# Attention in blocks of four heads: scores in strips of rows, keys copied by DMA, the sink as a column, normalised probabilities, a transposed value product

## What is computed

```python
q = einsum('bqm,muh->bquh', norm(x), Wq) + bq      # 32 heads of 64
k = einsum('bkm,mvh->bkvh', norm(x), Wk) + bk      # 8 heads of 64, each serves 4 query heads
v = einsum('bkm,mvh->bkvh', norm(x), Wv) + bv
q, k = rope(q) * SCALE, rope(k) * SCALE            # (even, odd) pairs are rotated
scores = where(abs(i - j) <= 128, q @ k.T, -1e9)   # 256 x 256 for each head
probs = softmax(concat([scores, sinks]))[..., :-1]
x = x + einsum('bquh,uhm->bqm', probs @ v, Wo) + bo
```

## Time and profile before

| | us |
|---|---|
| median of three runs | 1321.21 (1316.8 to 1321.73) |
| the profiled execution | 1318.92 |
| its span, first to last instruction | 1317.1 |
| TensorE busy | 1150.3 (87% of the span) |
| VectorE busy | 940.5 (71%) |
| ScalarE busy | 677.1 (51%) |
| GpSimd busy | 452.1 (34%) |

### The profile page before, as it was taken

How to read it: one execution, slowest core, us unless ns; L and a number is a source line. 1 busy time by engine, 2 the same in 40 slices (tenths; PEclk the granted TensorE clock), 3 DMA queues, 4 the chain that set the end, 5 groups by cost and what they waited for, 6 DMA issues and landing times. The chain is left out here.

```text
span 1317.1 us, 23131 instructions
## 1 busy us (share of the span) xinstructions
PE 1150.3 (87%) x7320; PEld 981.0 (74%) x7320; DVE 940.5 (71%) x2588; ACT 677.1 (51%) x1374; POOL 452.1 (34%) x393
## 2 busy tenths in 40 slices
PE   4899999999999897669998389999999989597667
PEld 3698998998999564558887278888888876476556
DVE  6789889889887456435555867767677673669983
ACT  1365655656666365123332266767767644144432
POOL 3746446446431333100000343334334310105730
PEclk9999999999999899579999699999999999788878
DMA  6000000000000400044442001011010100000001
GB/s 222 13 1 22 11 13 20 17 4 20 8 0 1 154 1 1 1 92 110 108 111 48 14 9 38 14 36 34 24 36 14 36 6 1 0 25 24 25 25 45
DMA packets 23497, 45.55 MB, mean 35 GB/s; under 512 B 3381, under 2 KB 10613, under 8 KB 23172
## 3 DMA queue, kind: packets, MB, share of 16 engines
q1 hardware_dynamic: 23428, 44.74, 12.3%
HBM read 43.09 MB, written 1.63 MB: 34 GB/s over the span
## 5 line engine op out<-in xcount | busy, mean ns | idle before, releaser
L421 ACT ACTIVATE sb_xT<-sb_a_nS,sb_a_nm 128x256 f32<-128x256 f32 x256 | 116.5, 504 | 67.8 <-DVE sb_a_nm L535 66.6
L673 PE MATMUL a_pO<-sb_a_v,sb_a_PT 128*128 (+1 forms) x1024 | 129.2, 269 | 0.0
L673 PEld LDWEIGHTS a_pO<-sb_a_v,sb_a_PT 128*128 128x128 f32 x1024 | 125.0, 192 | 0.0
L535 DVE CUSTOM_DVE_ANT_0 sb_a_nS<-a_pS,sb_a_mask,sb_a_nsink 128x256 f32<-128x256 f32 x256 | 113.1, 478 | 15.9 <-issue 7.7
L145 PE MATMUL a_pp<-sb_x_high,sb_a_w_low 128*128 128x512 f32 x224 | 98.8, 441 | 20.1 <-POOL sb_a_w_low L1612 8.4
L1684 ACT ACTIVATE sb_a_t<-a_pp,sb_a_w 64x512 f32<-64x512 f32 x128 | 87.5, 684 | 51.4 <-PE a_pp L145 50.6
L429 ACT COPY sb_a_PT<-a_pT 128x512 f32<-128x512 f32 x128 | 73.9, 577 | 33.7 <-PE a_pT L661 33.7
L145 PE MATMUL a_pp<-sb_x_low,sb_a_w_high 128*128 128x512 f32 x224 | 90.3, 403 | 0.0
L145 PE MATMUL a_pp<-sb_x_high,sb_a_w_high 128*128 128x512 f32 x224 | 90.2, 402 | 0.0
L145 PE MATMUL a_pY<-sb_a_wo_high,sb_a_OT_low 128*128 128x256 f32 x256 | 83.6, 326 | 6.4 <-DVE sb_a_OT_low L138 4.6
L661 PE MATMUL a_pT<-sb_ident,sb_xT 128*128 128x128 f32 x512 | 76.8, 272 | 5.3 <-ACT sb_a_PT L429 5.2
(11 more groups left out here) (351 smaller groups left out, 3651.1 us busy)
## 6 DMA issues: line engine op xcount, KB each, us to landing
sb_m_cw<-m_table SPq DMA_DIRECT2D x17, 512.0 KB
sb_f_w<-f_w SPq DMA_DIRECT2D x12, 384.0 KB, 3.0
sb_m_gu<-m_gu SPq DMA_DIRECT2D x17, 256.0 KB, 6.8
sb_a_w<-a_w SPq DMA_DIRECT2D x16, 257.0 KB, 2.9
sb_a_w<-a_w SPq DMA_DIRECT2D x8, 387.5 KB, 3.9
sb_a_wo<-a_wo SPq DMA_DIRECT2D x16, 192.0 KB, 2.4
sb_m_dn<-m_dn SPq DMA_DIRECT2D x17, 128.0 KB, 6.8
sb_a_wo<-a_wo SPq DMA_DIRECT2D x8, 256.0 KB, 2.7
```

What stands on the lines that cost most here:

```text
L421: out = nc.scalar.activation(Pm[u % 4][:, h, :], nS[u % 2][:, h, :], ACT.Exp, bias=nm[(u // 2) % 4][:, 2 * (u % 2) + h:2 * (u % 2) + h + 1 ...
L535: out = nc.vector.tensor_tensor_reduce(nS[u % 2][:, h, :], pS[u % 2][:, h * S:(h + 1) * S], wmask[:, j % 2, :], -1.0, nsink[par][:, c:c + ...
L673: out = nc.tensor.matmul(pO[j % 2][:, c0:c0 + A0_D + 1], PT[u % 2][:, h, c, :], values_at(G, 2 * b + c), start=(c == 0), stop=(c == 1))
```

## The change

The softmax, the sum over the heads and the products are the same. Changed are the blocks and the forms:

- A block is a batch b of a group: four heads, both tiles of query rows. There are 32 of them. The lags are one block (turning, weighing) and two (projecting). The loops are written out in full.
- Queries and keys are kept as even and odd components of four heads, 32 rows of each head. `scores(b)` is 16 float32 matmuls with 32 contraction rows (strip h for head h) and 256 columns, into a bank for each head. Nothing is split in parts, and there is no `kz`.
- Keys are projected once in the prologue (eight chunks), go to DRAM (`table`), and come back by DMA, with one head's 32 rows copied into all four strips (`keys_of`). In a group only four query chunks are left.
- The sink is column 256 of `nS`; `exps` writes 257 columns and gives the row sum through `accum_out`. `invert` takes its reciprocal, and GpSimd multiplies the probabilities by it (`normalise`).
- `weigh` has the values as the stationary operand (64 columns, two heads side by side in the array) and 256 moving columns of turned P, and writes the output already turned. `turn_O`, `shift`, `outputs` are gone; `high_OT` and `low_OT` work on 512 columns.
- `rope` makes two products a chunk, GpSimd makes the even and the odd component from four of them. Adding `bo` to x moves from VectorE to GpSimd.

Cut to its core (new lines only where all are new):

```diff
 @block.sync
+    sp.dma_start(wk, src["a0_wk"]).then_inc(wk_in, 16)      # 512 KB, ahead of w, a0 and wv
+    def keys_of(g, par):
+        for e in range(2):
+            sp.dma_start(kr[par][e][:, :], table[g, e].rearrange("(o d) t -> o d t", o=1).to_broadcast([A0_R, 32, T]))
+    for s in range(2):
+        sp.wait_ge(k_summed, 2 * s + 2)
+        for e in range(2):
+            sp.dma_start(table[4 * s:4 * s + 4, e], kall[s][e]).then_inc(table_out, 16)
...
+    for g in range(2, A0_G):
+        sp.wait_ge(scored, (g - 1) * NB)
+        keys_of(g, g % 2)
...
 @block.gpsimd
+    def rotate(n, out, done):
+        pool.wait_ge(roped, n + 1)
+        nc.gpsimd.tensor_tensor(out[0], tt[0], tt[3], ALU.subtract)
+        nc.gpsimd.tensor_tensor(out[1], tt[2], tt[1], ALU.add).then_inc(done, 1)
+    def normalise(G, par, b, h):
+        pool.wait_ge(rec_ready, G * (2 * NB) + (2 * b + h // 2 + 1))
+        part = Pm[b % 2][:, h, :, 0:S]
+        nc.gpsimd.tensor_tensor(part, part, rec[b % 2][:, h, :].rearrange("p (q o) -> p q o", o=1)
+                                .to_broadcast([P, 2, S]), ALU.mult).then_inc(normed, 1)
+    def body(G, par, first=False, last=False):
+        for b in range(NB):
+            if some(G, b, 1):
+                for h in (2, 3):
+                    normalise(g, par, bb, h)          # of block b-1
+            if b == 0:
+                w_low(G + 1, 1 - par); rotate_queries(G, par, 1); wo_low(G, par)
+            if b == 2 and not last:
+                rotate_queries(G + 1, 1 - par, 0)
+            for h in (0, 1):
+                normalise(G, par, b, h)
...
+    for t in range(NT):                               # after the rotations of the prologue
+        nc.gpsimd.tensor_tensor(k.x[:, t, :], k.x[:, t, :], bo[:, :], ALU.add).then_inc(bo_in, 1)
 @block.scalar
+    def exps(G, b, h):
+        act.wait_ge(maxed, I + (h + 1))               # in blocks 0 and 1 also: table_out 64
+        for qt in range(2):
+            out = nc.scalar.activation(Pm[b % 2][:, h, qt, 0:S + 1], nS[:, h, qt, 0:S + 1], ACT.Exp,
+                                       bias=nm[b % 2][:, h, qt:qt + 1], scale=-1.0,
+                                       accum_out=den[b % 2][:, h, qt:qt + 1])
+    def body(G, par, last=False):
+        for b in range(NB):
+            if some(G, b, 2):
+                high_OT(*lagged(G, b, 2))
+            if b == 0:
+                w_to_high(G + 1, 1 - par); wo_to_high(G, par)
+            for h in range(A0_R):
+                if some(G, b, 1):
+                    evac_PT(*lagged(G, b, 1), h)
+                exps(G, b, h)
 @block.vector
+    def rope(n, bias, even, free, free_at):
+        dve.wait_ge(proj, n + 1)
+        dve.wait_ge(free, free_at)                    # the rotation that last read tt
+        for tab, dst in ((cosq, tt[0 if even else 2]), (sinq, tt[1 if even else 3])):
+            out = nc.vector.scalar_tensor_tensor(out=dst, in0=a, scalar=bias, in1=row(tab), op0=ALU.add, op1=ALU.mult)
+    def body(G, par, first=False, last=False):
+        for b in range(NB):
+            if some(G, b, 2):
+                low_OT(*lagged(G, b, 2))
+            if b >= 1 and not last:
+                rope_queries(G + 1, 1 - par, b - 1)
+            if b == 0:
+                rope_queries(G, par, NB - 1); sink_column(G, par)
+            for h in range(A0_R):
+                maxima(G, par, b, h)                  # two of 256 columns each
+            invert(G, b, 0)
+            if some(G, b, 2):
+                add_y(*lagged(G, b, 2))
+            invert(G, b, 1)
 @block.tensor
+    def scores(G, par, b):                            # waits for maxima of block b-1
+        for qt in range(2):
+            for e in range(2):
+                for h in range(A0_R):
+                    strip = slice(32 * h, 32 * h + 32)
+                    c = b * S + qt * P
+                    out = nc.tensor.matmul(pS[h][:, qt * S:(qt + 1) * S], qT[par][e][strip, c:c + P],
+                                           kr[par][e][strip, b * S:(b + 1) * S], start=(e == 0), stop=(e == 1))
+    def weigh(G, b, p):
+        for c in range(2):
+            for h in range(2):
+                out = nc.tensor.matmul(pO[h * A0_D:(h + 1) * A0_D, p * S:(p + 1) * S], values_at(G, 2 * b + c),
+                                       PT[2 * p + h][:, c * S:(c + 1) * S], start=(c == 0), stop=(c == 1))
+    def body(G, par, last=False):                     # turn_P and weigh of b-1, project_out of b-2
+        for b in range(NB):
+            scores(G, par, b)
+            turn_P(g, bb, 0); project_out(g2, par2, b2, 0)
+            turn_P(g, bb, 1); project_out(g2, par2, b2, 1)
+            turn_P(g, bb, 2); chunk_part(n, ws[1 - par], b, 0, True, False)
+            turn_P(g, bb, 3); chunk_part(n, ws[1 - par], b, 1, False, True)
+            weigh(g, bb, 0); weigh(g, bb, 1)
+    for n, (kind, s, c) in enumerate(EARLY):          # 4 key, 4 query, 4 key chunks, banks pp and pY in turn
+        early_chunk(n, kind, s, c)
+        if n % 2 == 1:
+            values_of(n // 2)
```

More of the change, by code:

```diff
@@ L280, in attention_0 @@
-        rotated, rot_high, kr_low = sem("rotated"), sem("rot_high"), sem("kr_low")
-        bo_in, ones_set, rstd_ready, gate = sem("bo_in"), sem("ones_set"), sem("rstd_ready"), sem("gate")
-        NCH, KEYS = 6, 2
-        def chunk_at(G, par, u, last):
-            if u == 0:
-                return (G, par, NCH - 1)
-            return (G + 1, 1 - par, u // 2 - 1) if u % 2 == 0 and u < 2 * NCH and not last else None
-        def groups(eng, first, step, last):
-            first()
-            with eng.Fori(0, (A0_G - 2) // 2) as i:
-                for s in range(2):
-                    step(i * 2 + (1 + s), (1 + s) % 2)
-            last()
@@ L307, in part_of, with halves, chunk_no, sums_no @@
+        NB = B
+        def halves(G, each=16):
+            return each * (G // 2 + 1)
+        def chunk_no(G, c):
+            return 4 + c if G == 0 else 8 + 4 * G + c
+        def sums_no(G, half):
+            return 2 * G + half
+        def lagged(G, b, lag):
+            return (G, b - lag) if b >= lag else (G - 1, b - lag + NB)
+        def some(G, b, lag):
+            return G > 0 or b >= lag
         def part_of(tile, j):
             return tile[:, j // NH2, (j % NH2) * NC:(j % NH2 + 1) * NC]
+        def bank_of(n):
+            return pp if n % 2 == 0 or n >= 12 else pY
@@ L394, in _ @@
+            for G in range(A0_G):
+                body(G, G % 2, first=(G == 0), last=(G == A0_G - 1))
+            for h in (2, 3):
+                normalise(A0_G - 1, 1, NB - 1, h)
         @block.scalar
@@ L476, in _ @@
+            for G in range(A0_G):
+                body(G, G % 2, last=(G == A0_G - 1))
+            high_OT(A0_G - 1, NB - 2)
+            for h in range(A0_R):
+                evac_PT(A0_G - 1, NB - 1, h)
+            high_OT(A0_G - 1, NB - 1)
         @block.vector
@@ L605, in _ @@
-            dve.wait_ge(added, A0_G * NT)
+            for n, (kind, s, c) in enumerate(EARLY):
+                if kind == "k":
+                    rope_keys(n, s, c)
+                else:
+                    rope_queries(0, 0, c)
+                if n % 2 == 1:
+                    values(n // 2)
+            for t in range(len(EARLY) // 2, NT):
+                values(t)
+            for G in range(A0_G):
+                body(G, G % 2, first=(G == 0), last=(G == A0_G - 1))
+            low_OT(A0_G - 1, NB - 2)
@@ L665, in weigh @@
-            def weigh(G, par, u):
-                U, b, j, pair = G * A0_U + u, u // 4, u // 2, u % 2
-                pe.wait_ge(PT_ready, U + 1)
-                if pair == 0 and not (isinstance(G, int) and G == 0 and j < 2):
-                    pe.wait_ge(O_ready, G * NT + j - 1)
-                for h in range(2):
-                    c0 = (2 * pair + h) * (A0_D + 1)
-                    for c in range(2):
-                        out = nc.tensor.matmul(pO[j % 2][:, c0:c0 + A0_D + 1], PT[u % 2][:, h, c, :],
-                                               values_at(G, 2 * b + c), start=(c == 0), stop=(c == 1))
-                out.then_inc(pvd, 1)
@@ L698, in body @@
-            def body(G, par, first=False, last=False):
-                for u in range(A0_U):
-                    scores(G, par, u)
-                    if u >= 2 or not first:
-                        turn_P(G if u >= 2 else G - 1, (u - 2) % A0_U)
-                    if u >= 3 or not first:
-                        weigh(G if u >= 3 else G - 1, par if u >= 3 else 1 - par, (u - 3) % A0_U)
-                    if u % 2 == 0 and (u >= 6 or not first):
-                        turn_O(G if u >= 6 else G - 1, (u // 2 - 3) % NT)
-                    at = chunk_at(G, par, u, last)
-                    if at:
-                        chunk_of(*at)
-                    if u % 2 == 1 and (u >= 7 or not first):
-                        project_out(G if u >= 7 else G - 1, par if u >= 7 else 1 - par, ((u - 1) // 2 - 3) % NT)
```

(12 more changed lines are left out.)

614 lines of the change are left out of this document (281 added, 333 removed).

## The result

Over eight runs each, the changed kernel takes 1328.9 us (1325.3 to 1331.6) and the kernel before 1318.6 (1314.1 to 1321.9): a ratio of 1.0069, 95% interval 1.0053 to 1.0086. It is **0.7% slower**, where I forecast 1275 and gave slower 0.06. The profiled execution took 1329.8 us, its span is 1328.1.

The account below looks back on a forecast made before the run. VectorE's and ScalarE's order, not TensorE's work, was to set 10.5 us a block: 74.5 + 26 blocks (273) + 36 + tail 8.8 = 392.3 against 435.4, 43 less, so 1275 us; range 1238 to 1312.

Parts of the forecast that it names:

- The step that failed: SyncE's key copies, 1 MB a group, have some 40 us and cost nothing; without that cover 5 to 8 us a group.
- its neighbour: In the stage's start-up, the last keys' write, which ScalarE's first exponential waits for, is ready by 64 us and hidden.
- The ring: Per-block chain from weigh through high_OT, low_OT, rope, maxima, exponentials and turns back to weigh: 10.5 us against 12.2; chance 0.66.
- TensorE 8.9: TensorE's own work in a block sums to 8.9 us, the pace if nothing made TensorE wait.
- The first rival: The per-block chain is shorter than laid out and TensorE is the bound: 1233, or up to 1250 us; chance 0.12.
- Strips of 64 columns two at a time: In weigh, 16 records of 64 columns run in pairs: 8 slots, 1.76 us a block against 3.2 before.
- The slower rival: The two 64-column halves of weigh do not overlap: 8 slots more a block, 1330 us; chance 0.06.
- Strips in the program's order: Rival: TensorE's strips start strictly in order, scores 16 slots instead of 8, weighing 10: 1318 us, no change; chance 0.05.
- The sums' 0.1 each: The accumulated row sum adds 0.1 us to each ScalarE exponential, with bounds of 0 and about 0.3.
- GpSimd's normalisation at 1.04: Each of GpSimd's four normalisations a block takes 1.04 us, 1.29 as the other end; not a bound by itself.
- The prologue's 12 us later: Twelve chunks instead of five before the first scores, which start at 57.6 us instead of 45.6.
- Nothing changes behind the stage: The stages after the changed one keep their time, so the 43 us gained in the stage reach the total.

Follow-up runs that it names:

- the repaired version: Changed kernel with key copies and table writes in DMAs of 32 rows and the next weights issued ahead of the keys: 1257.5 us.
- Experiment 6: VectorE's rope moved behind the second head's maxima, against the kernel with strip DMAs and weights first (1257.5 us): 1245.1 us.
- experiment 7: Row sums of the exponentials dropped, probabilities not divided by them, against the kernel with strip DMAs and weights first (1257.5 us): 1254.9 us.
- Experiment 9: Head made the outermost loop in scores and weigh, same matmuls, against the kernel with strip DMAs and weights first (1257.5 us): 1343.3 us.

## Why the prediction was wrong

**The step that failed** is one sentence in the prologue's part: "SyncE's copies of keys (1 MB a group) wait for the block before last group's end and have some 40 us: nothing". With it goes its neighbour, "the write of the last keys ... is ready by 64, hidden". Two faults are in them.
- I priced the transfers by bytes and by the DMA share of the kernel before, as if 512 KB were 512 KB. The nearest row, 512 KB in 4.6 us, is a load of 128 partitions that shared the engines with all else in flight. The new ones get 105 GB/s together, however idle the rest is: six in a row are 30 us, and the write was ready at 85.8 and not at 64. Already the first write took 16.1 us.
- I asked who needs the keys, and by when, but not who is behind them. The next group's weights stand there on SyncE and are needed one block after their issue. Their landing went from 2.9 to 14.5 us. My sentence even has the price "without that cover" (5 to 8 us a group, measured 7.4 at each boundary), but for the wrong transfer: I gave the cover to the keys, and the weights had none.

The cost of that step: 46.5 us at the boundaries and 23.7 at the start (third block 100.9, against 77.2 with the DMAs mended, 74.5 forecast), 70 together; the repaired version is 71 us faster than the changed kernel and 61 faster than the one before.

**The other steps.**
- *The ring*: right in kind and near in size, 9.9 against 10.5. In the trace TensorE idles 0.59 before the third turn with ScalarE's copy as releaser. The terms that were too long: a rope product is 0.66 from start to start (I took 0.77 from rows of 64 partitions), and the hand-overs and the small differences of the other terms come to 0.4 less in all. The last block with the tail behind it took 20.1 (431.4 to 451.6), where I had 8.8 and 8.8: 2.5 too short. Experiment 6 shows the rope's place in the ring (and that the scores take it over, as the prediction had said), 7 the sums'.
- *TensorE 8.9*: not contradicted. Scores 1.94 and weighing 1.88 are 1.76 with 0.12 to 0.18 for the change of form, as taken; the four turns, with what stands behind each, were never seen shorter than 5.5 (mine: 5.1), but ScalarE paced them wherever I looked. The first rival, TensorE the bound, did not come: the ring was shorter than I laid it out by 0.6 of the 1.6 that it needed.
- *Strips of 64 columns two at a time*: right, 16 records in 1.88 to 1.95. The slower rival that I named (no overlap, 1330) gave about the measured time for a reason that did not occur. A time that fits is no proof of its story; the block of 9.9 rejects it at once.
- *Strips in the program's order* (1318): its 16 slots for the scores are rejected by the same rows. These rows would still fit an order by whole calls, of two records each, since the head is innermost. Experiment 9 rejects that too and shows the limit: a strip's first record starts at 383.03, before the fourth call of the strip ahead. By the Trainium skill, "TensorE: Matmul & The Clock Gate", Part 3, starts would be in order; the trace of experiment 9 does not agree, though with the head outermost the time comes nearer to it.
- *The sums' 0.1 each*: 0.09 from start to start (0.50 in place of 0.41). Left out, they gave back 0.26 a block and not 0.36 (experiment 7).
- *GpSimd's normalisation at 1.04*: measured 1.04, and it sets nothing.
- *The prologue's 12 us later*: 57.6 forecast, 57.2 with mended DMAs.
- *Nothing changes behind the stage*: the rest is 5 us shorter. Of that, 4 are the cross-attention, which took 98.8 us in place of 103.1. TensorE's first products there, in the changed kernel,

```profile
452.25 7.10 PE L1068 MATMUL x_pS<-sb_ctxT,sb_x_w 128*128 128x512 f32 x16 [1.42 <-PEq L226]
```

  took 8.80 in the kernel before, at a granted clock of 0.81 over those 8.8 us (1.00 here). There TensorE had been busy all of the 48 us from 382 to 430, at 1.00, and here it is idle in a part of every block. Whether that is the reason was not tested: versions with the same blocks took 97.7 to 102 for that stage, so the exact place where the clock falls is not settled.

## What to carry to other kernels

Price a DMA by its shape, not by its bytes: ask how many of the 16 engines it can use, and look for a DMA share that stands still at a round fraction (0.25) while everything waits. When a transfer "has 40 us", list what is queued behind it, and price those with their own due times. And when the parts of a block are shown to be faster and the stage is not, count the periods over the whole stage: a steady 9.9 hid six blocks of 17.5.

## What the runs showed of the hardware

- A DMA with a first dimension of 4 on its DRAM side (as source or as destination) moved 105 GB/s at a DMA share of 0.25 and held up what was issued behind it (weights that landed in 14.5 us in place of 2.9); by strips of 32 rows the same bytes went at 234 GB/s and a share of 1.01, and the weights behind them landed in 3.7. Four DMAs in the place of one, with the first dimension still 4, left the share at 0.26.
- Strips of TensorE's array run ahead of the program's order, by about three records: 32 score records in 1.94 us with the head innermost, in 4.8 with it outermost; 16 weighing records in 1.9 with four of one half in a row.
- The accumulated sum of an exponential on ScalarE is an instruction of its own of 0.19 to 0.20 us, of which 0.09 show from start to start; without four of them in the ring a block was 0.26 shorter.
- The same stage behind took 97.7 to 103.1 us with its code unchanged. In the kernel before the granted clock was 0.81 over its first 8.8 us, in experiment 7 it fell to 0.50 about 19 us in: 4 us that hide a gain of 7 in a total.
